# A recommender layer: the last tile of 128 samples run by itself, with transposes by TensorE; the row blocks of each group moved through HBM

## What is computed

```python
embed = tables[arange(26)[None, :], sparse_inputs]      # 2048 x 26 x 32
p   = einsum('bfe,bge->bfg', embed, embed)              # pair sums
l_z = einsum('bfe,feh->bh', embed, w_z)                 # 26*32 -> 256
l_p = einsum('bfg,fgh->bh', p, w_p)                     # 26*26 -> 256
l_1 = relu(concat([l_z + l_p + l_b, dense_inputs]))
h   = relu(l_1 @ W1 + b1)                              # 269 -> 128
y   = sigmoid(h @ Wf + bf)                              # 128 -> 1
```

## Time and profile before

| | |
|---|---|
| median of three runs | 599.03 us (598.78 to 599.04) |
| span of the profiled execution, first to last instruction | 548.8 us |
| around the span, median less span | 50.2 us |
| POOL busy | 409.0 us (75%), 430 instructions |
| DVE busy | 417.5 us (76%) |
| ACT busy | 139.7 us (25%) |
| PE busy | 131.1 us (24%) |

### The profile page before, as it was taken

How to read it: one execution, slowest core, us unless ns; L and a number is a source line. 1 busy time by engine, 2 the same in 40 slices (tenths; PEclk the granted TensorE clock), 3 DMA queues, 4 the chain that set the end, 5 groups by cost and what they waited for, 6 DMA issues and landing times.

```text
span 548.8 us, 1701 instructions
## 1 busy us (share of the span) xinstructions
PE 131.1 (24%) x204; PEld 48.0 (9%) x204; DVE 417.5 (76%) x250; ACT 139.7 (25%) x333; POOL 409.0 (75%) x430
## 2 busy tenths in 40 slices
PE   0000000415334100060465100051433600005067
PEld 0000000201111000020121000020110100002023
DVE  4204199998992369998996419999899547999995
ACT  0000004404551021704452010340455110250323
POOL 6777777777777777777777777777777777777792
PEclk9999999976567555585666655567665555558569
DMA  6222323122122222222112222222112222312220
GB/s 148 21 14 13 13 13 14 13 13 14 14 13 13 13 13 14 13 14 13 13 14 14 13 13 13 13 14 13 14 13 13 14 14 13 14 13 13 13 46 2
DMA packets 19640, 9.56 MB, mean 17 GB/s; under 512 B 9888, under 2 KB 19629, under 8 KB 19629
## 3 DMA queue, kind: packets, MB, share of 16 engines
q0 software_dynamic: 13312, 6.84, 22.4%
q1 hardware_dynamic: 6318, 2.63, 2.1%
HBM read 8.85 MB, written 0.01 MB: 16 GB/s over the span
## 4 chain that ended last, share of the span: by engine, by line
POOL 69%; issue 23%; DVE 6%; DMA 1%; PE 1%; ACT 0%; ACTq 0%; POOLq 0%; DVEq 0%
POOL rows L286 66%; DVE pairs L368 3%; DVE prod L348 2%; POOL prod L302 2%; POOL prod L313 1%; DMA rows<-in_L_rec_tables,which 1%; PE ps_h L643 0%; DMA raw<-in_r_sparse_inputs 0%; DVE pair_rows L404 0%; PE ps_h L680 0%; ACT scores L551 0%; PE ps_copy L692 0%; ACT hidden L537 0%; ACTq L120 0%; DVE pairs_T L395 0%
## 5 line engine op out<-in xcount | busy, mean ns | idle before, releaser
L286 POOL DMA_INDIRECT rows<-in_L_rec_tables,which x416 | 393.5, 946 | 128.4 <-issue 125.8
L348 DVE TENSOR_TENSOR prod<-ps_copy,rows 128x1664 f32<-128x1664 f32 (+12 forms) x103 | 194.2, 1910 | 16.8 <-ACT ps_copy L471 16.8
L368 DVE TENSOR_REDUCE pairs<-prod 128x76 f32<-128x2432 f32 (+13 forms) x73 | 195.3, 2680 | 0.0
L626 PE MATMUL ps_h<-field_rows,wz 128*128 128x512 f32 x96 | 59.4, 784 | 290.3 <-ACT field_rows L482 285.4
L379 DVE STREAM_TRANSPOSE rows_T<-rows 128x512 f32<-128x512 f32 (+1 forms) x28 | 18.6, 663 | 98.1 <-DMA rows<-in_L_rec_tables,which 90.7
L471 ACT COPY ps_copy<-rows 128x128 f32<-128x128 f32 (+2 forms) x63 | 21.2, 336 | 273.3 <-DMA rows<-in_L_rec_tables,which 273.0
L643 PE MATMUL ps_h<-pair_rows,w_pair 96*128 96x512 f32 (+2 forms) x64 | 50.2, 943 | 100.3 <-ACT pair_rows L505 84.4
L482 ACT COPY field_rows<-rows_T 32x512 f32<-32x512 f32 (+1 forms) x112 | 58.7, 524 | 34.9 <-DVE rows_T L379 33.4
L626 PEld LDWEIGHTS ps_h<-field_rows,wz 128*128 128x128 f32 x96 | 23.8, 258 | 328.0 <-issue 292.1
L505 ACT COPY pair_rows<-pairs_T 32x256 f32<-32x256 f32 (+1 forms) x96 | 33.5, 349 | 63.1 <-DVE pairs_T L391 61.9
L643 PEld LDWEIGHTS ps_h<-pair_rows,w_pair 96*128 96x128 f32 (+2 forms) x64 | 17.7, 296 | 130.4 <-ACT pair_rows L505 71.9
(11 more groups left out here) (37 smaller groups left out, 31.7 us busy)
## 6 DMA issues: line engine op xcount, KB each, us to landing
rows<-in_L_rec_tables,which POOLq DMA_INDIRECT x416, 3.4
wz<-in_L_rec_w_z SPq DMA_DIRECT2D x1, 768.0 KB, 5.8
field_rows<-rows_T SPq DMA_DIRECT2D x16, 32.0 KB, 1.9
w_pair<-in_w_low SPq DMA_DIRECT2D x1, 288.0 KB, 5.4
w_back<-in_w_high SPq DMA_DIRECT2D x1, 288.0 KB, 5.7
raw<-in_r_sparse_inputs SPq DMA_DIRECT2D x1, 156.0 KB, 2.2
w<-in_L_rec_W SPq DMA_DIRECT2D x1, 128.0 KB
dense_in<-in_r_dense_inputs SPq DMA_DIRECT2D x1, 104.0 KB, 3.2
```

What stands on the lines that cost most here:

```text
L286: nc.gpsimd.indirect_dma_start(rows[:, r % 2, f, k, :], None, table_rows, bass.IndirectOffsetOnAxis(ap=which[:, t, f:f + 1], axis=0),).the ...
L348: ins = nc.vector.tensor_tensor(products(r, s)[:, 0:tiles, at:at + g + 1, :], own.broadcast_to([P, tiles, g + 1, E]), rows[:, r % 2, 0:g + ...
L368: nc.vector.tensor_reduce(pairs[:, 0:tiles, first:end], products(r, s)[:, 0:tiles, :, :], AX.X, ALU.add)\
L626: ins = nc.tensor.matmul(ps_h0[:, h, :], wz[:, j, h * P:(h + 1) * P], field_rows[:, j, :, :, :].rearrange("p q t b -> p (q t b)"), start=( ...
```

## The change

The order of the batch stays, and so does the number of gathers. Four things differ.

1. **The last group is cut in three phases**: tiles 0 and 1, tile 2, tile 3 (`PHASES = 6`, `TILE_RANGE`; `END` is the phase of the last tile). POOL gathers the 26 fields of a phase before it goes to the next. Tiles 0 to 2 of the group share the layout of the other groups with 384 columns (`ABREAST`, `WIDTH`); the last tile has its own rows, products and pair sums, laid in the buffer of `rows` that group 2 has left.
2. **The last tile is transposed by TensorE** (`turn_solo`, through the one PSUM buffer 3 of `ps_copy`), brought back to SBUF by ACT (`lay_solo`), summed over 128 columns (`sum_solo`) and taken through layers of 128 columns. POOL multiplies 8 pairs of field 24 and 12 of field 25 for this tile alone, where it had all of field 24 and half of field 25.
3. **All row blocks of all groups go through HBM** on SP's queue (four writes to `passage`, then one read to `field_rows`); `lay_rows` is gone from ACT.
4. **Units and stages** are of two fields from field 10 or 12 on; ACT and DVE skip every second wait for a buffer. The pair blocks of the first three groups are transposed and laid as one move of three blocks; those of the last group (tiles 0 to 2) one by one.

The core of the diff:

```diff
-FINE = [(0, 4), (4, 6), (6, 8), (8, 10), (10, 12)] + [(f, f + 1) for f in range(12, 26)]
+PHASES = GROUPS + 2
+PLAIN = [(0, 4), (4, 8), (8, 12)] + [(f, f + 2) for f in range(12, 26, 2)]
+ENDING = [(0, 4), (4, 8), (8, 12)] + [(f, f + 2) for f in range(12, 22, 2)] + [(f, f + 1) for f in range(22, 26)]
...
-    PAIR_MOVES = [(0, 2), (2, 3), (TAIL, TAIL + 1)]
+    PAIR_MOVES = [[(0, 3), (TAIL, TAIL + 1)]] * (GROUPS - 1) + [[(c, c + 1) for c in range(TAIL + 1)]]
+    TILE_RANGE = [(0, K)] * (ROUNDS - 1) + [(0, 2), (2, K - 1), (K - 1, K)]
+    ABREAST = [K] * (ROUNDS - 1) + [K - 1]
+    TURNS = [("rows", 0), ("rows", 1), ("rows", 2), ("rows", 3), ("pairs", 0), ("rows", 4), ("pairs", 1),
+             ("rows", 5), ("rows", 6), ("pairs", 2), ("pairs", 3)]
+    POOL_24 = 8
+    POOL_25 = 12
...
+            for r in range(ROUNDS):                       # SP
+                n = ABREAST[r]
+                for j in range(MOVED):
+                    sp.wait_ge(rows_turned, CH * r + j + 1)
...
+                    for q in range(QUADS):
+                        sp.dma_start(passage[j, :, :, q, 0:n * Q].rearrange("u e x -> e u x"),
+                                     rows_T[Q * q:Q * (q + 1), j, :, 0:n, :].rearrange("p u k b -> p u (k b)"))\
+                            .then_inc(passed[j], DMA)
...
+                    sp.wait_ge(passed[j], DMA * QUADS * (r + 1))
+                    sp.dma_start(field_rows[:, j, :, 0:n, :].rearrange("p q k b -> p q (k b)"),
+                                 passage[j, :, :, :, 0:n * Q].rearrange("u e q x -> (u e) q x")).then_inc(rows_in[j], DMA)
...
+            def lay_solo(what, c):                        # ACT
+                n = TURNS.index((what, c))
+                act.wait_ge(solo_turned, n + 1)
+                if what == "rows":
+                    nc.scalar.copy(solo_T[0:chunk_rows(c), n, :], ps_copy_bank(SOLO_COPIES)[0:chunk_rows(c), 0:P])\
+                        .then_inc(solo_laid, 1)
...
+            for u, (first, end) in enumerate(UNITS[END]):  # ACT, last tile
+                copy_fields(END, u)
+                if first == 0:
+                    lay_last_rows(r)
+                    lay_last_pairs(r)
+                if first == 4:
+                    lay_solo("rows", 0)
+                    make_hidden0(r)
+                if first == 8:
+                    lay_solo("rows", 1)
+                    make_hidden1(r)
+                if first == 12:
+                    make_scores(r)
...
+            def turn_solo(what, c):                       # PE
+                n = TURNS.index((what, c))
+                if n == 0:
+                    pe.wait_ge(multiplied, STAGES_BEFORE[END])
+                else:
+                    pe.wait_ge(solo_laid, n)
...
+                nc.tensor.transpose(ps_copy_bank(SOLO_COPIES)[0:wide, 0:P], came, ident[:, :]).then_inc(solo_turned, 1)
...
+            def sum_solo(what, c):
+                n = TURNS.index((what, c))
+                pe.wait_ge(solo_laid, n + 1)
+                if n == 0:
+                    pe.wait_ge(hidden0_made, HALVES * ROUNDS)
...
+                for h in range(HALVES):
+                    ins = nc.tensor.matmul(ps_h0[:, h, 0:P], weights[:, h * P:(h + 1) * P], came, start=(n == 0), stop=last)
...
+            turn_solo("rows", 6)
+            turn_solo("pairs", 2)
+            sum_solo("pairs", 2)
+            turn_solo("pairs", 3)
+            sum_solo("pairs", 3)
+            sum_solo_h1()
+            sum_solo_logit()
```

More of the change, by code:

```diff
@@ L598, in _ @@
[L598 to L603 removed]
+                    lay_solo("rows", 1)
+                    make_hidden1(r)
+                if first == 12:
+                    make_scores(r)
+                if first == 14:
+                    lay_solo("rows", 2)
+                if first == 16:
+                    lay_solo("rows", 3)
```

632 lines of the change are left out of this document (327 added, 305 removed).

## The result

The changed kernel took 620.01 us (618.56 to 621.12, four runs) beside 598.9 us for the kernel before: ratio 1.0357, 95% interval 1.0341 to 1.0374, slower by 21.1 us. Forecast were 596.7 us and a range of 593.0 to 601.0. The profile from which the forecast was made must come from such a chip: its span is 548.8 us, and the spans of the kernel before are 548.3 to 549.3 us on the two chips of that kind and 595.6 to 597.6 us on the three others.

The account below looks back on a forecast made before the run. POOL's gathers make up the chain before, with DVE the bound from 425 us after the change. DVE's never-waiting work, waits for ACT, tail and store gave span 546.5; plus 50.2 around it, 596.7 us, range 593.0 to 601.0.

Parts of the forecast that it names:

- Sum: 546.5 + 50.2 around the span.: Whole kernel: span of 546.5 us plus 50.2 us around it gives 596.7 us, 2.3 under the median of 599.03.
- Last start again 522.5, cost 0.: POOL's gathers: as many in another order, so the last again starts at 522.5 us, at cost 0.
- These two need no clock, only ACT's order: Entering the last tile: DVE waits 1.0 and 3.0 us for field copies standing behind ACT's small copies.
- Waits in tile 2 and at the last tile's start 1.4, 1.0, 3.0 and 2.6 us: DVE's waits for ACT's copies: tile 2, then fields 0 to 3, 4 to 7 and 8 to 11 of the last tile.
- The 2.6: Fields 8 to 11, last tile: DVE waits 2.6 us, the copy standing behind `make_hidden0` and PE's tail block at low clock.
- The never-waiting end, 529.8: DVE's last group: 103.9 us of work from 425.3, never waiting for other engines, ends at 529.8 us with its own-result waits.
- DVE's last sum 538.3: End of DVE's last sum: 531.2 us plus 7.1 us of waits in the last tile, against 539.3 before.
- Last sum to store 6.4: Tail from DVE's last sum to the store: 6.4 us against 7.8 before, between 5.0 at high and 6.9 at low clock.
- Rival A: High clock through the last tile: waits 5.3 us, tail 5.0, span 543.3, time 593.5 us; chance 0.20.
- SP's cover of 3 us: Row blocks through HBM on SP's queue: stays ahead of PE by 3 us at the last chunk.
- one of the signs of being wrong: Wrong if DVE awaits a landing in the last tile, its starting waits are under 1 us, or PE awaits `field_rows` after 505.
- Rival C: Way through HBM late: PE gets the last chunk's fields at 512 instead of 505, 602 us; chance 0.09.

Follow-up runs that it names:

- the profile of 543.9 us: The changed kernel, unaltered, run again on a chip where the kernel before takes 550.45 us: 545.91 us, ratio 0.992.

## Why the prediction was wrong

*"Sum: 546.5 + 50.2 around the span."* This step failed first: the term of 50.2 us. The page's 548.8 us and the median of 599.03 are not one execution with 50 us around it; every run here has 1.7 to 2.2 us around its span (the one with nothing behind its gathers 12.4), also those of 551 us. Where the kernel before takes 598.4 us, 2.1 are around the span and 47.5 are inside it, as slow steps and late signals. The page is of a chip on which gathers keep 1.25 us, the times are of chips on which they do not: 598 to 599 us on three chips, 551 us on two. I saw the 50 us and gave them a name instead of asking what in the profile could be 50 us longer.

*"Last start again 522.5, cost 0."* Right at one pace (522.45), wrong at the other (559.40). By itself this would have moved both kernels alike.

*"These two need no clock, only ACT's order"*, with copies at 0.28 us. This is the step that turned the order round. On the slow chips a small copy goes every 1.40 us and a signal comes 2.5 to 17 us late, until about 587 us: the wait of 3.0 us was 16.82. I had priced 66 more DVE instructions, 24 small copies and the chain of turned blocks by their length and a hop of 0.05 us. The kernel before has only its last layers behind this moment, 8.3 us; the changed one had its last tile there, 31.3 us.

Where the premise held, the working can be compared term by term, in the profile of 543.9 us. POOL done at 530.5: 529.45. Waits in tile 2 and at the last tile's start 1.4, 1.0, 3.0 and 2.6 us: 1.30, 0.41, 3.00 and 1.34, and the fifth, 0.5, did not come. The 2.6 was mis-sized by the clock: the tail block, from 511.73 us on, took 1.45 us for 4 matmuls where 2.8 was taken from the earlier trace rows; the granted clock was 1.00, the 2.4 GHz level, over 511 to 514 us, not the 0.5 forecast. The never-waiting end, 529.8, was 530.9 (536.97 less 6.05). DVE's last sum 538.3: 536.97. Last sum to store 6.4: 5.14, though the granted clock was 0.50 there:

```profile
511.00:514.00 3.00, 2.38 (x10) 1.22 (x8) 1.61 (x5) 1.51 (x5) 2.17 (x3) 1.00 0.22 13
...
536.00:544.00 8.00, 4.46 (x15) 2.92 (x15) 1.32 (x3) 1.69 (x5) 0.00 (x0) 0.50 0.00 1
```

These are stretches of it: busy us and count of PE, weight loads, DVE, ACT and POOL, then the granted clock, two lines as in the earlier trace rows. Span 546.5: 543.9. A gain of 2.3 us was forecast, 4.5 measured. Of the 2.6 us of span the last sum makes 1.3 and the tail 1.3. That is nearer to Rival A, whose sum gives a span of 543.3 us with the wait of 1.3 that was measured; its tail of 5.0 us fits by luck, since it was put down to the high clock and ran at 0.50. SP's cover of 3 us at the last row block was not there either: PE waited 0.55 us for this load at 508.93, after 505, one of the signs of being wrong that the prediction names.

Rival C, the way through HBM, was the main rival for a slower kernel. In the kernel before it costs 2.2 us at one pace and gains 1.8 at the other, and it is not the loss. No rival had chips of two paces, nor a step between short instructions that has nothing to do with their length.

What stays open: what it is behind a gather that is cleared in 1.40 us, whether it belongs to the kernel or to its recording, and why two chips of five do not show it. The 20 outstanding gathers and the 14 free instructions are worked out from steps in time, not read from a counter. That TensorE's transpose at 570.12 was really done then, and only its signal late, rests on the record, whose ends are modelled.

## What to carry to other kernels

Set the span of the profiled execution against the timed runs before anything else: about 2 us around it is normal here, and 50 us meant that profile and times were of different conditions, so that its rows did not price the timed kernel. Where short instructions of several engines start at one fixed step apart, whatever their length, count instructions and signals, not microseconds of work, and look at how much is left to do when this ends. This plan for the last tile gains where DVE waits for gathers (15 us with gathers 1.7 us apart) and loses where the last tile stands behind late signals (21 us).

## What the runs showed of the hardware

- The same kernel took 598 to 599 us on three chips and 550 to 551 us on two, within 0.3% on each. Gathers alone: 584.6 and 530.4 us, one run each, and in both the rows of the last group had landed 4.10 us after the last gather's start.
- On the slower ones, 416 gathers issued 1.25 us apart fall to 1.40 us from 216 to 238 us on; from 238 us on the mean step is 1.40 us. With gathers 1.70 us apart in the mean the two kinds of chip differ by 1.2 us of 739.
- On the slower ones, until 582 to 588 us, short instructions on ACT, POOL and DVE start 1.40 us apart (0.70 at times), on ACT after some 14 without this step, and a wait for another engine's finished instruction was released up to 17 us after the end in the record.
- With nothing but gathers, the slower chip issued its store at 561.42 us, its span ended 10.8 us later, and the execution took 12.4 us more than its span; on the other it was 1.8 and 2.2 us.
